# Identity matmuls in TensorE's pauses of the first batch, and an earlier start for GpSimd's split of a weight

## The reference, cut to what matters

```python
x = L0_attn_video                                     # (8, 512, 256)
x = x + _layernorm(_L0_attn_ref(_layernorm(x), ...))
x = x + _layernorm(_L0_ffn_ref(_layernorm(x), ...))
...
qp = softmax_kernel(q, proj, is_query=True)           # exp(xp - diag - stab) + eps
kp = softmax_kernel(k, proj, is_query=False)
k_sum = jnp.sum(kp, axis=2)
denom = jnp.einsum('bhnm,bhm->bhn', qp, k_sum)
ctx = jnp.einsum('bhnm,bhnd->bhmd', kp, v)
out = jnp.einsum('bhnm,bhmd->bhnd', qp, ctx) / denom[..., None]
attn = out.transpose(0, 2, 1, 3).reshape(b, n, d) @ Wo.T + bo
x = layer_norm(video + attn, g2, be2)
ff = jax.nn.relu(x @ W1.T + b1) @ W2.T + b2
return layer_norm(x + ff, g3, be3)
```

## Time and profile before

| what | value |
|---|---|
| median of 3 runs | 816.89 us (816.01 to 818.01) |
| the profiled execution | 815.45 us, its span 813.7 us |
| TensorE busy | 697.6 us (86%) |
| VectorE busy | 619.1 us (76%) |
| ScalarE busy | 470.5 us (58%) |
| GpSimd busy | 365.8 us (45%) |
| mean granted TensorE clock | 0.924 of full speed |

### The profile page before, as it was taken

The page is one execution under the profiler, slowest core; times in us unless marked ns, Lnnn a source line. Parts: engine busy times, 40 slices in busy tenths (PEclk is TensorE's granted clock), DMA queues, the critical chain, the costliest instruction groups (busy, mean ns, idle before and its releaser), DMA issues. The chain is left out here.

```text
span 813.7 us, 15543 instructions
## 1 busy us (share of the span) xinstructions
PE 697.6 (86%) x5701; PEld 566.2 (70%) x5701; DVE 619.1 (76%) x1282; ACT 470.5 (58%) x749; POOL 365.8 (45%) x364
## 2 busy tenths in 40 slices
PE   3888999999999999999999979433699999999920
PEld 3756868768768768768778668332488889998820
DVE  4867758978978878898798687778767677767681
ACT  3644755875866867857857745363155544445560
POOL 4235334545536527517616514200345466554673
PEclk9889999999999999999999999655599999999975
DMA  8000010021011011011011111330236664555694
GB/s 248 28 2 2 1 52 2 1 79 54 27 52 52 26 52 52 26 52 52 29 48 29 53 54 52 114 103 0 79 99 149 155 146 111 118 144 157 177 224 96
DMA packets 50703, 61.00 MB, mean 75 GB/s; under 512 B 9313, under 2 KB 44897, under 8 KB 50657
## 3 DMA queue, kind: packets, MB, share of 16 engines
q1 hardware_dynamic: 42400, 46.45, 17.5%
q0 software_dynamic: 7296, 13.77, 9.0%
q10 hardware_dynamic: 960, 0.17, 0.1%
HBM read 39.28 MB, written 21.10 MB: 74 GB/s over the span
## 5 line engine op out<-in xcount | busy, mean ns | idle before, releaser
L2051 PE MATMUL pF<-w,h 128*128 128x256 f32 x448 | 106.1, 383 | 0.0
L1093 POOL DMA_INDIRECT kp<-row_scratch,idx_g x32 | 41.6, 1299 | 117.1 <-issue 60.3
L2051 PEld LDWEIGHTS pF<-w,h 128*128 128x128 f32 x448 | 81.9, 190 | 13.1 <-issue 3.4
L871 ACT ACTIVATE h<-pX,b1cur 128x512 f32<-128x512 f32 x64 | 44.2, 690 | 62.6 <-DVE b1cur L1836 45.7
L2440 PE MATMUL pX<-w_lo,h_hi 128*128 128x256 f32 x256 | 73.2, 286 | 0.8 <-issue 0.8
L960 POOL TENSOR_SCALAR ve<-mv 128x4 f32<-128x4 f32 x36 | 8.5, 235 | 144.7 <-DVE mv L1171 143.8
L2440 PE MATMUL pX<-w_hi,h_lo 128*128 128x256 f32 x256 | 72.5, 283 | 0.0
L2440 PE MATMUL pX<-w_hi,h_hi 128*128 128x256 f32 x256 | 72.5, 283 | 0.0
L1792 DVE TENSOR_TENSOR h_lo<-h,h_hi 128x512 fp32r<-128x512 f32 x64 | 42.9, 690 | 28.9 <-ACT h_hi L863 28.9
L1101 POOL DMA_INDIRECT acc_scratch<-qp,idx_s x28 | 53.1, 1897 | 22.7 <-DVE qp L1818 18.4
L1988 PE MATMUL pX<-x2T_hi,w_lo 128*128 128x512 f32 x128 | 51.4, 402 | 1.6 <-DVE x2T_lo L1862 1.6
(11 more groups left out here) (403 smaller groups left out, 2080.8 us busy)
## 6 DMA issues: line engine op xcount, KB each, us to landing
kp<-fc1T SPq DMA_DIRECT2D x8, 1024.0 KB, 7.3
w<-fc2T SPq DMA_DIRECT2D x8, 1024.0 KB, 8.3
xin<-video SPq DMA_DIRECT2D x8, 512.0 KB, 3.6
x<-video SPq DMA_DIRECT2D x7, 512.0 KB, 4.5
out<-x SPq DMA_DIRECT2D x7, 512.0 KB, 3.0
acc_scratch<-xf SPq DMA_DIRECT2D x7, 512.0 KB, 2.9
row_scratch<-y SPq DMA_DIRECT2D x7, 512.0 KB, 3.0
kp<-acc_scratch SPq DMA_DIRECT2D x4, 512.0 KB, 5.2
```

The lines of the kernel that those rows point to most:

```text
L871: nc.scalar.activation(h[:, n, :], pM[n % M_SLOTS], ACT.Gelu_apprx_tanh, bias=b1cur[:, n:n + 1]).then_inc(he_ready, 1)
L1093: pool.indirect_dma_start(xg[:, g, :], None, row_d, bass.IndirectOffsetOnAxis(ap=idx_g[:, g:g + 1], axis=0)).then_inc(gathered, 16)
L2051: ins = nc.tensor.matmul(pF[m][:, half * D:(half + 1) * D], h[:, k, tok(2 * m + half)], w2[:, k, :], start=(k == 0), stop=(k == FC - 1))
```

## The change

TensorE gets a helper `keep_busy(bank, count)` that multiplies the 128 by 128 identity by itself in float32, `count` times, into a PSUM bank that nothing reads before it is written anew. It is called 49 times over: 20 before `turn_x(0)`, 4 behind it, one before 6 of the 8 chunks of `fold_of_hidden`, 8 before `turn_tops`, 5 behind it, 2 before `sums_of_keys`, 4 behind `turn_context`. The two parts of `fold_of_hidden` become chunks 0 to 3 and 4 to 7, and the first one waits for `bias_ready` in addition, since pF[1] is still read until then. The wait for `qp_ready` goes from the end of `turn_context` to the start of `all_heads`, behind the last four identity matmuls. GpSimd's wait for `cx_ready` becomes one for `xl_ready` at `2 * C`.

```diff
                     pool.wait_ge(fold_ready, 2)
-                    pool.wait_ge(cx_ready, 1)
+                    pool.wait_ge(xl_ready, 2 * C)
...
+            def keep_busy(bank, count):
+
+                for _ in range(count):
+                    nc.tensor.matmul(bank[:, 0:P], ident[:], ident[:], start=True, stop=True)
+
...
                     ins.then_inc(a_ready, 1)
+
+                def all_heads():
                     pe.wait_ge(qp_ready, (i + 1) * G)
-
-                def all_heads():
                     pe.wait_ge(cx_ready, i + 1)
...
                 def fold_of_hidden(n0, n1):
                     if n0 == 0:
+                        pe.wait_ge(bias_ready, 1)
                         pe.wait_ge(w1_in, 16)
                         pe.wait_ge(wff_in, 16 * N_WFF)
                     for n in range(n0, n1):
+                        if n < 4 or n % 2 == 0:
+                            keep_busy(pF[1], 1)
...
-                    fold_of_hidden(0, 6)
+                    fold_of_hidden(0, 4)
                     features(0, J_XQ + 1, qT, 1)
                     spread_kmax()
-                    fold_of_hidden(6, FC)
+                    fold_of_hidden(4, FC)
+                    idle = slot_a(0, J_CTX)
                     turn_x(1)
+                    keep_busy(idle, 8)
                     turn_tops()
+                    keep_busy(idle, 5)
                     features_turned(0)
                     context()
+                    keep_busy(slot_a(0, J_KSUM), 2)
                     sums_of_keys()
                     features_turned(1)
                     turn_context()
+                    keep_busy(slot_a(0, J_DEN), 4)
                     all_heads()
...
             pe.wait_ge(const_ready, N_CONST)
+            keep_busy(pA[0], 20)
             turn_x(0)
+            keep_busy(pA[0], 4)
             batches(pe, body)
```

## The result

The changed kernel took 810.86 us (median of 4 runs, 808.87 to 811.93) where the kernel before took 816.49 (median of 4, 816.01 to 818.01): ratio 0.9922, 95% interval 0.9909 to 0.9934. I had said 810.1 in a range of 807.8 to 813.8. The profiled execution is the fastest of the four, 808.87 us with a span of 807.1; against the span before, 813.7, that is 6.6 us less, and my sum was 6.8.

A forecast was written before the change was run, and what follows sets the result against it. It took step 0's serial chain of TensorE, VectorE and ScalarE, with slow-clock stretches and waits, to be the bound. 3.6 us to the heads plus 3.2 at attention's end made 6.8: 810.1 us, range 807.8 to 813.8.

The forecast's parts named there:

- Start: Before and in `keys`: some 0.65 us earlier start plus 1.3 saved in `keys`, sum 1.95 (bounds -0.5 and 2.2).
- up to 0.5 us late: At the start: the first transposes begin at 10.79, or up to 0.5 us later behind the twenty identity matmuls.
- Price of one: One float32 identity matmul: 0.26 us at 2.4 GHz and 0.485 at 1.2 GHz, taken from transposes.
- Fold and `turn_tops`: `fold_of_hidden` to `turn_tops`: second part ends 0.2 us late, shift falls to 1.75; `turn_tops` can start at 38.86.
- The margin I gave as 0.2 us: Before `turn_tops`: eight identity matmuls end about 38.7, `turn_tops` can start at 38.86, so hidden by 0.2 us only.
- To the heads: `turn_tops` to `all_heads`: first turned features at 40.9, second at 47.0, shift 3.6 us.
- The two end at 46.0: Before `sums_of_keys`: two identity matmuls (0.5 us) end at 46.0, then sums of about 1 us.
- GpSimd: GpSimd's split runs from 47.0 to 60.5, before `aT_lo` at 61.1: free by 0.6 us.
- Attention's end: `attention_out` to step 1: one wait of 1.43 us gone, the rest the clock; gain 3.2 us (bounds 1.4 and 3.2).
- The sum: Whole kernel: 3.6 to the heads plus 3.2 at attention's end, 6.8 us, giving 810.1.
- offset of 1.44 us: Whole kernel before: the median of the runs is 1.44 us above the profiled execution, added to the forecast.
- rival A: In `fold_of_hidden`: the clock still falls and identity matmuls delay `turn_tops`; gain 3.6 us, 813.3; chance 0.17.

The follow-up runs named there:

- e9: The changed kernel measured again, no edit but an empty line less: 811.31 us.
- e10: The changed kernel with four identity matmuls instead of eight before `turn_tops`: 811.02 us.
- e8: The changed kernel with ten identity matmuls instead of twenty at the start: 811.87 us.
- e3: The changed kernel cut back to the 20 and 4 identity matmuls around `turn_x(0)`, old fold and GpSimd's old wait: 814.92 us.
- e5: The changed kernel without the six identity matmuls inside `fold_of_hidden`: 812.77 us.
- e6: The changed kernel with all 49 identity matmuls cut from 128 columns to one: 821.97 us.
- e7: The changed kernel with sixteen identity matmuls instead of eight before `turn_tops`: 813.02 us.
- e1: The kernel before with only GpSimd's wait changed, no identity matmuls: 814.66 us.
- e2: The changed kernel with all 49 identity matmuls but GpSimd's old wait for `cx_ready`: 812.23 us.
- e4: The changed kernel with only the 25 identity matmuls from the fold to `all_heads`, none at the start, GpSimd's old wait: 815.96 us.

## Why the prediction was right

**Start.** The 20 ended at 9.77, and at 9.33 to 10.65 over the traces with 20 of full width, before the 12.65 of twenty cold ones. `keys` came 0.64 earlier (0.65) and was 1.34 shorter (1.3). That the transposes may come up to 0.5 us late is worked out from no row and shown by no run: they began at 10.62 to 10.90 in those traces, against 10.79 before, in e9 and e10 without a pause behind the identities. e8, with half the identities, lost 1.07 us at `all_heads`. e3's 2.3 us don't show the price of the start, since its trace carried only 0.86 to the heads.

**Price of one.** I took 0.26 us warm, from transposes. The rows say 28.65 - 28.43 = 0.22, about the lower value of 0.23. Cold, it was (41.94 - 38.53) / 8 = 0.43 in e5 instead of 0.485. This was mis-sized, and it changed little, since nearly all were hidden in the profile.

The Trainium skill (TensorE: Matmul & The Clock Gate, "LDWEIGHTS (loading the stationary operand)") puts the two loads of one at an estimated 0.21 us and names no clock. Warm, the trace agrees, 0.22; cold it doesn't: with one column, where there is nearly nothing but the loads, e6 took 0.43.

**Fold and `turn_tops`.** `turn_x(1)` waited as expected for a fold that ended a little late, and `turn_tops` started at 38.92 (38.86). The margin I gave as 0.2 us was 0.46, by the cheaper identities. What goes beyond the pause is on the path, e7 shows.

**To the heads.** The first turned features came at 40.99 (40.9), the second at 47.24 (47.0), `all_heads` at 51.28 (51.05): shift 3.38 instead of 3.6. The step that gave 0.2 back is "The two end at 46.0", said of the two identities ahead of the sums: they ran from 45.54 to the start of the sums at 46.19, 0.65 us where I had taken 0.5. VectorE's sum of the keys ended as `rest_of_x` began, at 45.78, so the two held the path by up to 0.4 us.

**GpSimd.** Start 47.27 (47.0), end 60.31 (60.5), `aT_lo` at 61.30 (61.1), free by 1.0 us. Shown by e1 and e2 from both sides.

**Attention's end.** 6.14 - 2.83 = 3.3 us (3.2). Alone, GpSimd's wait did all of it in the profile of e1. With the wait for `aT_lo` but no fall `attention_out` took 4.57 (e3) and 4.63 us (e4): of the 3.3 us some 1.75 are the wait's and 1.55 the clock's. The clock fell behind the pause that the wait made in the traces of the kernel before and of e2, and not in those of e3 and e4, so the second part is won only in executions that would have had that fall.

**The sum.** 3.4 + 3.3 = 6.7 against 3.6 + 3.2 = 6.8. The offset of 1.44 us between the profiled execution and the median was 1.99 after. That is most of what lies between 810.1 and 810.86, and there the picture in the prediction, one likeliest case with the others beside it, was too plain. The rival A (clock lost in the fold) is not another outcome for the kernel, it is one that some executions have: of the seven traces with the six fold identities four show a fall behind the fold (e4, e7, e9, e10), three don't (the changed kernel, e2, e8). In e9 it cost 0.8 us at `all_heads`, not the 3.2 that I priced, because the fall came late, behind the fold, and ended within the eight. The forecast was what one profile shows, and it is partly luck that it was this one: it is the fastest of its four and has neither fall, as the profile of the kernel before has no fall behind 476. The profiled execution of e9, the same program, is 815.45 - 811.51 = 3.9 us under the kernel before, not 6.6. Nor is the clock all of the spread: executions of the kernel before with one and the same mean clock of 0.924 took 815.34 to 817.80 us.

What stays open: why a fall comes in one execution and not in the next. No experiment controls it. That the fall behind 476 costs 1.4 us is read from two things that go together in 13 traces; no edit has tested it. What makes executions with the same mean clock differ by 2 us is not known either.

## What to carry to other kernels

Before filling a pause with idle matmuls, find what ends it, and fill less than it lasts at the low clock, not at the high one: eight ahead of a pause fit with 0.46 us to spare at 2.4 GHz, delayed the work behind it by 0.8 to 1.0 us where the clock had fallen (e9, e4); four did not (e10), though the medians don't tell the two apart. Look at a stretch of one-column matmuls as at a pause: the clock fell behind it here though TensorE was busy all through. A long GpSimd instruction costs most where VectorE's two-input instruction on the critical path meets it; its start is worth choosing for what it will lie beside when the rest has moved. And read more than one trace when the clock decides: the same program had it and lost it. A median that comes out as forecast doesn't show the route (e3); the trace does.

## What the runs showed of the hardware that I had not expected

`csum_own`, an instruction of 8 elements with two SBUF inputs, took 704 ns at most before and 0.17 us at 51.26 in the changed kernel, although a multiplication of GpSimd (54.22 to 59.91, and 47.27 to 52.95) lay beside it both times. It took 0.70 or 0.71 in the four traces where it came 0.4 us behind the start of the first of the two multiplications, and 0.17 in eight others, beside the second. In e6 it met GpSimd's rounding instead, and was held until that ended. VectorE's and GpSimd's timelines of e6:

```profile
62.67 1.58 DVE L1260 TENSOR_TENSOR csum_own<-csum,epsmask 128x8 f32<-128x8 f32 x1
```

```profile
62.34 1.89 POOL L1046 CAST w_hi<-h 128x2048 fp32r<-128x2048 f32 x1
```

62.67 + 1.58 = 64.25, and 62.34 + 1.89 = 64.23. The first `aT_lo` before, 2.40 us long from 64.68 on, ended at 67.08, 0.55 us behind the end of the subtraction of `w1_lo`. GpSimd's timeline of the kernel before:

```profile
61.95 4.58 POOL L1048 TENSOR_TENSOR w_lo<-h,w_hi 128x2048 fp32r<-128x2048 f32 x1
```

The Trainium skill (GPSIMD Engine Reference, "1. Specifications") names the clash but makes no difference between GpSimd's instructions. By these traces the rounding (once, in e6) and the subtraction (in four traces) hold a VectorE instruction with two SBUF inputs until they end, the multiplication by a column for up to about 1.1 us from its start (54.64 + 0.70 - 54.22). Why they differ is not shown. Nor does every such pair clash: two batches later in the kernel before, `csum_own` took 0.17 us at 170.99, 0.09 behind the start of a GpSimd instruction of two inputs and 4 elements (1.04 us). GpSimd pays too: its addition for `b2_b` took 1.19 us beside the second `aT_lo` and 0.76 without it.
